# Side work ahead of each branch of PE on the maxima flags, the branch turned round, and chunk by chunk waits in the flagged maxima

## The reference, cut to what matters

```python
# x: (4, 2048, 256), f32; 16 heads of 16
x = x + attn_a(layernorm(x))   # causal softmax attention, scale 1/4
x = x + ffn(layernorm(x))      # shift mix with mu; sigmoid(xr W_r) * (relu(xk W_k)^2 W_v)
x = x + attn_b(layernorm(x))   # keys: decaying scan over t, normed, scaled by exp(10 key_scale)
x = x + ffn(layernorm(x))      # values: mix with the next one, normed, scaled; queries are
                               # the keys shifted by one; causal softmax; W_c
return x
```

## Time and profile before

| what | us |
|---|---|
| median of 3 runs | 3423.64 |
| lowest and highest | 3422.43, 3432.76 |
| the profiled execution's own time | 3428.78 |
| its span | 3427.0 |
| PE busy | 3151.7 |
| ACT busy | 2291.9 |
| DVE busy | 1423.6 |
| POOL busy | 850.3 |

### The profile page before, as it was taken

How to read it: one execution, slowest core, us unless ns; L and a number is a source line. 1 busy time by engine, 2 the same in 40 slices (tenths; PEclk the granted TensorE clock), 3 DMA queues, 4 the chain that set the end, 5 groups by cost and what they waited for, 6 DMA issues and landing times.

```text
span 3427.0 us, 51952 instructions
## 1 busy us (share of the span) xinstructions
PE 3151.7 (92%) x19172; PEld 1212.5 (35%) x19172; DVE 1423.6 (42%) x3534; ACT 2291.9 (67%) x2487; POOL 850.3 (25%) x1278
## 2 busy tenths in 40 slices
PE   7999999999999789997999999999999989899897
PEld 4222233333333333332333333333333333333334
DVE  5222235545454542434233333445445545422434
ACT  2788767777676467674667676776777764688462
POOL 4111123333222222221222221323233221322111
PEclk9999999999999899998999999999999998999899
DMA  5222212222221123222212222121222211222111
GB/s 139 78 74 67 83 43 68 68 66 67 57 65 48 53 59 85 63 59 62 79 55 71 74 79 86 54 59 52 69 64 67 71 52 37 62 63 75 41 44 44
DMA packets 229682, 223.05 MB, mean 65 GB/s; under 512 B 33221, under 2 KB 212933, under 8 KB 229320
## 3 DMA queue, kind: packets, MB, share of 16 engines
q1 hardware_dynamic: 228504, 217.47, 22.2%
q10 hardware_dynamic: 816, 0.79, 0.1%
HBM read 146.80 MB, written 71.32 MB: 64 GB/s over the span
## 4 chain that ended last, share of the span: by engine, by line
PE 77%; DVE 10%; issue 7%; ACT 4%; POOL 1%; SPq 1%; DMA 1%; ACTq 0%; DVEq 0%; POOLq 0%
PE ps L1055 26%; PE ps L1013 25%; PE ps L875 12%; PE ps L866 10%; ACT probs L810 4%; DVE pmax L1349 2%; PE ps L860 2%; DVE ln_st L1121 1%; DVE xn L1130 1%; DVE o_blk L1391 1%; POOL v_st L691 1%; DVE x_buf L1242 1%; PE ps L903 0%; DVE nw_u L1111 0%; DVE nw_u L1113 0%
## 5 line engine op out<-in xcount | busy, mean ns | idle before, releaser
L810 ACT ACTIVATE probs<-ps 128x1024 f32<-128x1024 f32 x2176 | 2136.5, 1023 | 749.8 <-PE ps L1013 555.8
L1013 PE MATMUL ps<-q_st,k_st 99*128 99x512 bf16 (+3 forms) x5120 | 1204.3, 353 | 120.6 <-issue 103.5
L1055 PE MATMUL ps<-probs,v_st 128*17 128x512 f32 (+3 forms) x10240 | 1163.1, 535 | 41.9 <-ACT probs L810 16.2
L713 POOL TENSOR_SCALAR_AFFINE_SELECT probs<-probs 128x256 f32<-128x256 f32 (+1 forms) x896 | 423.4, 487 | 1705.9 <-ACT probs L810 1700.4
L1013 PEld LDWEIGHTS ps<-q_st,k_st 99*128 99x128 bf16 x5120 | 424.0, 98 | 1062.4 <-ACT probs L810 467.8
L1055 PEld LDWEIGHTS ps<-probs,v_st 128*17 128x17 f32 x10240 | 185.0, 96 | 534.5 <-issue 355.6
L1391 DVE STREAM_TRANSPOSE o_blk<-ps 128x512 f32<-128x512 f32 x128 | 90.8, 710 | 449.4 <-PE ps L1055 449.4
L866 PE MATMUL ps<-xT,wT 128*128 128x512 f32 x512 | 255.6, 625 | 1.6 <-issue 1.0
L1242 DVE TENSOR_TENSOR x_buf<-x_buf,ps 128x512 f32<-128x512 f32 x64 | 43.4, 679 | 380.1 <-PE ps L875 380.1
L637 POOL TENSOR_TENSOR parts<-rest,parts 128x512 bf16<-128x512 f32 x96 | 119.9, 1249 | 260.8 <-DVE parts L1153 260.8
L1266 DVE SCALAR_TENSOR_TENSOR buf_v<-buf_v,ps 128x512 f32<-128x512 f32 x64 | 44.0, 687 | 304.8 <-PE ps L875 304.8
(11 more groups left out here) (136 smaller groups left out, 2152.0 us busy)
## 6 DMA issues: line engine op xcount, KB each, us to landing
part_a<-parts SPq DMA_DIRECT2D x192, 128.0 KB
x_buf<-in_L_attn_a_X SPq DMA_DIRECT2D x32, 512.0 KB, 4.5
q_st<-part_a SPq DMA_DIRECT2D x128, 128.0 KB
o_chan<-o_out SPq DMA_DIRECT2D x64, 256.0 KB, 2.4
o_in<-o_chan SPq DMA_DIRECT2D x64, 256.0 KB, 4.5
q_st<-part_b SPq DMA_DIRECT2D x128, 128.0 KB
k_st<-part_a SPq DMA_DIRECT2D x64, 192.0 KB, 2.9
part_b<-parts SPq DMA_DIRECT2D x96, 128.0 KB
```

The costliest lines, as they stand in the source:

```text
L713: last = pool.affine_select(out=o, in_=o, compare_op=ALU.is_ge, fill=0.0, base=0, pattern=[[0, o.shape[1]], [1, P]], channel_multiplier=-1)
L810: nc.scalar.activation(probs[:, g % NP_BUF, :], ps[:, bk:bk + 2, :].rearrange("p a n -> p (a n)"), ACT.Exp, scale=SCALE[ATT[g // (NHG * NG ...
L1013: last = pe.matmul(o[:, col:col + w], k_st[0:KROWS, j, kb * P:(kb + 1) * P], q_st[0:KROWS, j, qc * CH + q0:qc * CH + q0 + w], start=True, ...
L1055: last = pe.matmul(ps[32 * j:32 * j + VW, bank, q0:q0 + w], v_st[:, k % 2, kb, hg * HG + j, :], p, start=(kb == 0), stop=(kb >= TB * qc), ...
```

## The change

Three things, all in PE's program and in the table of due times.

1. `FRONT` is -4, one slot ahead of the branch. The jobs `MA` and `MB` that were due at an instance's start - 3 are due at start - 4 now, with all their parts on all engines. The `P` jobs of the second batch start so that u2 falls in that slot: 19 slots before the instance and not 8 after it. The first jobs begin 10 slots earlier.
2. The branch is turned: the body of the unflagged case comes first in the code, and the flagged one stands in `Else`.
3. In the flagged maxima the waits for queries and keys of a chunk stand before the first piece that needs the chunk, and no longer all ahead of the head flags.

```diff
+FRONT = -AHEAD - 1
...
-    jobs = [Job("P", 0, c, 0, -80 + 14 * c) for c in range(NCH)]
+    jobs = [Job("P", 0, c, 0, -90 + 14 * c) for c in range(NCH)]
     for c in range(NCH):
-        jobs.append(Job("P", 1, c, 1, start(0, c) + 8))
+        jobs.append(Job("P", 1, c, 1, start(0, c) + FRONT - T_P["u2"]))
     for k, b in ((1, 0), (2, 1), (5, 2), (6, 3)):
-        jobs += [Job("MA", b, c, k + 1, start(k, c) - 3) for c in range(NCH)]
+        jobs += [Job("MA", b, c, k + 1, start(k, c) + FRONT) for c in range(NCH)]
     for k, b in ((3, 0), (4, 1)):
         for c in range(NCH):
-            jobs.append(Job("MB", b, c, k, start(k, c) - 3))
+            jobs.append(Job("MB", b, c, k, start(k, c) + FRONT))
             jobs.append(Job("P", b + 2, c, k + 1, start(k, c) + 29))
-    jobs += [Job("MB", 2, c, 7, start(7, c) - 3 if c < 3 else start(7, 2) + 32) for c in range(NCH)]
+    jobs += [Job("MB", 2, c, 7, start(7, c) + FRONT if c < 3 else start(7, 2) + 32) for c in range(NCH)]
...
-FIRST_SLOT = -100
+FIRST_SLOT = -110
...
                 for i, (qb, b0, nb) in enumerate(MAX_PIECES):
+                    if qb % TB == 0:
+                        pe.wait_ge(s_q[qb // TB], 16 * (len(Q_RUNS) + 1) * (n + 1))
+                        pe.wait_ge(s_k[qb // TB], 16 * len(K_RUNS) * (n + 1))
...
-                for c in range(NCH):
-                    pe.wait_ge(s_q[c], 16 * (len(Q_RUNS) + 1) * (n + 1))
-                    pe.wait_ge(s_k[c], 16 * len(K_RUNS) * (n + 1))
...
-                with pe.If(any_flag > 0):
-                    maxima(n)
-                    slots(n * NG - AHEAD, (n + 1) * NG - AHEAD, True)
-                with pe.Else():
+                with pe.If(any_flag == 0):
                     pe.sem_inc(s_mx["scores"], NMP * HG)
                     pe.sem_inc(s_mx["turned"], HG)
                     slots(n * NG - AHEAD, (n + 1) * NG - AHEAD, False)
+                with pe.Else():
+                    maxima(n)
+                    slots(n * NG - AHEAD, (n + 1) * NG - AHEAD, True)
```

## The result

| kernel | us, median | runs | us in the profiled execution's span |
|---|---|---|---|
| before | 3427.7 | 4 | 3427.0 |
| changed | 3535.6 (3527.2 to 3542.0) | 4 | 3540.3 |

What follows compares the result with a forecast made beforehand. PE, busy for 92% of the span, was taken as the bound, with 142 us of branch waits to attack. Gains less losses summed to 96 us saved from 3428.8: profiled 3333, median 3328, range 3297 to 3388.

Steps and rivals of the forecast that it cites:

- (a): Ahead of PE's flag branches: a queued projection covers the wait; the twelve and nine ordinary waits save 29.3 and 12.9 us.
- (b): On POOL: the value product runs ahead of both masks, so products in twelve instances stop waiting; 10.4 us saved.
- (c): At PE's turned branch: no far jump behind flagged bodies saves 22.4 us; dropping the last flagged body saves 1.9.
- A: At PE's branch: the flag load waits for an empty queue, so queued work covers nothing; about 3404 us, chance 0.12.
- B: At PE's turned branch: a second code fetch on 28 branches; about 3473 us, slower than before, chance 0.08.
- (f): On DVE: o1's residual and layernorm move ahead of taking the last chunk's output; 12 us lost, ends 0 and 27 x 3.
- Rival C: On DVE: its flag branch or the reordering takes longer, costing 40 to 70 us; about 3380 us, chance 0.11.
- (g): At the start: second-batch parts ahead of the first branch delay first scores, 2.5 us lost; cover in instances 1 to 3 saves 1.5.
- (d): Into flagged instances: two far jumps, but no wait for all queries and keys; 4 us lost, ends -4 and +16.
- (e): PE's granted clock: shorter branch waits avoid most time at the lower clock level behind them; 36 us saved.

Runs made afterwards that it cites:

- e6: e5 with POOL's value product one slot earlier, ahead of the masks of groups 63 and 64; 3340.9 us, ratio to before 0.974 to 0.978.
- e9: The kernel before with only o0 moved ahead of the branch and the first jobs ten slots earlier; 3374.0 us, ratio to before 0.983 to 0.987.
- e3: The kernel before with the two bodies of PE's branch exchanged and nothing else; 3420.7 us, ratio to before 0.998.
- e2: The changed kernel with t0 alone one slot later; 3451.3 us, ratio to before 1.006 to 1.010.
- e5: e4 with the second batch's projection jobs back at their old slots; 3356.7 us, ratio to before 0.978 to 0.981.
- e8: The changed kernel with only the second batch's projection jobs back at their old slots; 3518.2 us, ratio to before 1.026 to 1.029.
- e10: e6 with the two bodies of PE's branch exchanged, as in the changed kernel; 3343.7 us, ratio to before 0.975 to 0.978.
- e1: The changed kernel with all ffn job parts except o0 and the loads back in their slots of before; 3380.3 us, ratio to before 0.985 to 0.989.
- e4: e1 with the branch as it was before the change; 3375.7 us, ratio to before 0.984 to 0.987.

## Why the prediction was wrong

**Right.** The reading of the 32 branch waits: flag load and branch run in PE's sequencer while queued work goes on. The twelve and nine ordinary waits were put at 1.2 us each; in the changed kernel they lie between 1.3 and 2.1 us with two longer ones (2.6, 3.9), and in e6 mostly between 1.2 and 1.9. They fell by 30 us in sum where (a) had 42. The late masks (b) were sized nearly right: the POOL waits vanished, and e6 found 15.8 us where 10.4 were put. The three waits behind flagged instances went (c). Rivals A and B are both out, A by e9 (cover alone, 52 us less), B by e3.

**The step that failed is (f).** It saw that o1's layernorm goes ahead of the taking, and that t0 runs in a bank which is taken late, and priced only t0's own wait, at 0.98 us. That one measured 1.45. The next reader of the same bank, chunk 1's products, isn't mentioned: before, t0 was not in their bank. They need DVE's copy of t0, which stands behind layernorm and two takings, and that is 27 x 2.75 = 74 us, and at 1.5 us of clock behind 22 of them an estimated 33 us: some 107 us that the sum doesn't have (e2 gave 84 of it back, and kept a wait of 1 us ahead of 27 products). It also missed the transposes of the second layernorm, which moved a slot too (16 x 0.87 = 14 us). Rival C had the right engine, DVE, and 2 to 3 us in each of the 27 instances, but looked for them at t0 and not at the products behind it. Its price was 40 to 70 us, without the clock; it ended at 3400, still faster than before, so no rival with DVE in it reached what was measured.

**(g), mis-sized.** 2.5 us lost less 1.5 won; e5 and e8 measure 17 to 19 us lost. The term had layernorm waiting for the flags' cast. It waits for a load of SP, which sits behind part stores in SP's row, so layernorm starts at 97.1 us and not at 89.6. It had the copies and the projections, but at the full clock.

**(d), mis-sized.** 4 us lost were put, with ends of -4 and +16; the four waits rose by 11.0, inside these ends. With it goes the gain of (c): the two together were put at 20 us won. The turn alone gave 5.5 us (e3) and none with cover (e6 to e10); the chunk waits gave 17.

**(e).** The clock was given back at most branches (1.00 behind the wait of 1.79 us, and behind 12 others of the 17), and lost again behind the new wait. Where the new wait is absent it stays won: e10 has the cover, the turned branch, the chunk waits and POOL's early value product, without the shifts of (f) and (g). PE is busy 34 us less in it than before, where 36 were put. It measured 82 us below before (3425.6 to 3343.7), where the terms (a) to (e) add up to 109; the first three rows below split that.

| term | put at | measured in |
|---|---|---|
| cover and clock, (a) and (e) | 78 us won | before to e9: 52 won |
| POOL, (b) | 10 won | e5 to e6: 16 won |
| turn and chunk waits, (c) and (d) | 20 won | e9 to e5: 17 won; e6 to e10: 3 lost |
| (a) to (e) together | 109 won | e10: 82 won |
| (f), shift of o1, t0 and DVE | 12 lost | changed to e1: 155 lost |
| (g), start | 1 lost | e8: 17 lost |

The 155 are against e1, which has POOL's wait back; with it they are an estimated 170.

**The price of a far jump.** With one far jump more ahead of them, the four waits into flagged instances rose by 17.8 us in e3, 4.5 us each; the three instances that were reached over two far jumps, 7.5 us idle each, are reached without one, and no score wait of 0.3 us is left there. The Trainium skill (Advanced Engine Details and Errata, Control Flow Timing) has about 51 ns for a jump and 108 ns for compare-and-branch; by e3 the figures are no price for a jump into code far away. The Trainium skill (Runtime: NRT & Kernel Launch, Instruction fetch mechanics) says that a taken branch to a target outside the current window stalls until its page is fetched; the waits of e3 agree, though no row here shows the fetch itself.

## What to carry to other kernels

Work queued ahead of a data-dependent branch covers the sequencer's load and jump for about as long as it lasts, so one projection ahead of each was worth 1.5% here (e9). But move that one piece alone: when a due-time table shifts a whole job by a slot, list for every part which buffer it gets in its new slot, who needs that buffer next, and where the release stands in the other engine's row. And a wait put down to "issue" may be a semaphore wait in the sequencer: look for the instruction of another engine that ended a tenth of a microsecond before.

## What the runs showed of the hardware

Without work queued behind the last release, a branch with a far jump kept PE idle for up to 4 us, and turning it moved that time and did not remove it (e3). Queued work hides at most its own duration: o0 occupies PE for 1.99 us, and in the changed kernel the 21 ordinary waits are 1.4 us shorter in the mean; with 3.0 us of matmuls queued, 1.3 to 1.9 us of idle time stay in most instances. One wait of 3.9 to 5.0 us stands among the ordinary ones in the changed kernel and in e1, e2, e4, e5 and e6, not always in the same instance; no run shows why.

Not expected was what the granted clock did behind waits as short as these. Behind all 27 waits of 2.75 us in the changed kernel the granted clock was 0.50 to 0.62 in the 3 us that followed. Behind its 17 branch waits of 1.3 to 1.9 us it was 1.00 in 13 cases and 0.69 to 0.77 in four. The two groups differ in more than the length: PE had idled another 1.45 us at t0, four microseconds ahead of the long waits. The first matmuls behind a wait don't tell it: in the kernel before, the two at 634.40 took 0.59 us, their full-clock duration, behind a wait of 3.55 us, and the granted clock of the 3 us from there was 0.66.
